# Relational graph layers on one core: sums kept relation by relation, read by TensorE from the ring, and the last node tile in a bank of its own

## The reference

```
agg = segment_sum(x[src], etype * N + dst)          # per relation and node, 8 x 3125 x 256
h   = relu( sum_r agg[r] @ W[l, r] + x @ root[l] + bias[l] )   # layers 1 and 2
h   = sigmoid( ... )                                 # layer 3
x   = x + h3 + linear_attention(layernorm(x))
x   = x + mixture_of_8_experts(layernorm(x), top 2)
```

## Time and profile before

| what | us |
|---|---|
| median of three runs | 3841.38 |
| the profiled execution | 3845.77 |
| its span, from the first to the last instruction | 3844.0 |
| TensorE busy | 3026.0 (79%) |
| GpSimd busy | 2399.1 (62%) |
| VectorE busy | 1830.8 (48%) |
| ScalarE busy | 689.2 (18%) |

### The profile page before, as it was taken

The page is one execution under the profiler, slowest core; times in us unless marked ns, Lnnn a source line. Parts: engine busy times, 40 slices in busy tenths (PEclk is TensorE's granted clock), DMA queues, the critical chain, the costliest instruction groups (busy, mean ns, idle before and its releaser), DMA issues.

```text
span 3844.0 us, 55574 instructions
## 1 busy us (share of the span) xinstructions
PE 3026.0 (79%) x15306; PEld 2475.6 (64%) x15307; DVE 1830.8 (48%) x3744; ACT 689.2 (18%) x1109; POOL 2399.1 (62%) x2536
## 2 busy tenths in 40 slices
PE   2888788888768888888888677877877884899991
PEld 2767667676657677776777566776766761566661
DVE  5455554554545555455454365565555542222222
ACT  0111111111111111111111122122222221222220
POOL 3777777777757777777776577777777755000005
PEclk9788988888978877788787788788878877899996
DMA  4333333433443333333333433333333325333334
GB/s 149 114 113 115 114 113 113 117 113 113 117 123 109 109 107 107 109 108 108 109 108 102 146 106 104 105 105 105 106 105 105 105 80 197 104 105 105 106 113 129
DMA packets 205784, 434.65 MB, mean 113 GB/s; under 512 B 51647, under 2 KB 115608, under 8 KB 205674
## 3 DMA queue, kind: packets, MB, share of 16 engines
q0 software_dynamic: 120864, 330.20, 30.0%
q1 hardware_dynamic: 81424, 102.07, 8.1%
q10 hardware_dynamic: 3386, 1.24, 0.1%
HBM read 398.24 MB, written 35.09 MB: 113 GB/s over the span
## 4 chain that ended last, share of the span: by engine, by line
POOL 46%; PE 22%; issue 21%; DMA 4%; DVE 3%; DVEq 1%; ACT 1%; SPq 1%; ACTq 0%; POOLq 0%
POOL arena L473 44%; PE bank L1293 7%; PE bank L1411 4%; PE bank L1438 4%; PE bank L1236 4%; DMA arena<-rows_dram,arena 2%; POOL xs_dram L507 1%; PE bank L1423 1%; POOL arena L518 1%; DMA hT_all<-in_L_ffn_b_dram 1%; PE bank L1231 1%; DVEq L973 1%; PE bank L1229 1%; DMA arena<-in_L_gnn_roots_dram 0%; DVE arena L987 0%
## 5 line engine op out<-in xcount | busy, mean ns | idle before, releaser
L473 POOL DMA_INDIRECT arena<-rows_dram,arena x2418 | 2289.9, 947 | 848.6 <-issue 783.2
L1293 PE MATMUL bank<-arena 128*128 128x128 f32 x9672 | 1756.4, 329 | 578.5 <-DVE arena L987 309.8
L1293 PEld LDWEIGHTS bank<-arena 128*128 128x128 f32 x9672 | 1526.3, 229 | 823.2 <-DVE arena L987 429.4
L987 DVE TENSOR_TENSOR arena<-arena,bank 128x256 f32 x2418 | 1019.2, 422 | 1385.6 <-PE bank L1293 1076.7
L1236 PE MATMUL bank<-arena 128*128 128x256 f32 x2400 | 612.6, 397 | 0.0
L1236 PEld LDWEIGHTS bank<-arena 128*128 128x128 f32 x2400 | 457.4, 203 | 52.0
L571 ACT COPY arena<-arena 128x1024 f32<-128x1024 f32 x150 | 300.8, 2053 | 607.1 <-DVE arena L928 308.1
L518 POOL DMA_INDIRECT arena<-ys_dram,pos x50 | 48.5, 969 | 511.0 <-DMA ys_dram<-arena 496.1
L958 DVE TENSOR_TENSOR arena<-bank,arena 128x1408 f32<-128x1408 f32 x222 | 355.9, 1604 | 15.4 <-issue 15.2
L1123 DVE TENSOR_TENSOR hT_all<-bank,hT_all 128x512 f32<-128x512 f32 x114 | 73.7, 687 | 342.6 <-DMA hT_all<-in_L_ffn_b_dram 284.8
L1411 PE MATMUL bank<-arena 128*128 x456 | 211.3, 607 | 11.7 <-issue 11.4
(11 more groups left out here) (188 smaller groups left out, 1100.6 us busy)
## 6 DMA issues: line engine op xcount, KB each, us to landing
arena<-rows_dram,arena POOLq DMA_INDIRECT x2418, 2.8
hT_all<-b_dram SPq DMA_DIRECT2D x58, 512.0 KB, 3.5
arena<-in_L_ffn_W_dram SPq DMA_DIRECT2D x16, 512.0 KB, 7.6
arena<-in_L_ffn_W_dram SPq DMA_DIRECT2D x8, 1024.0 KB, 13.6
arena<-xs_dram SPq DMA_DIRECT2D x59, 128.0 KB, 3.6
hT_all<-in_L_ffn_b_dram SPq DMA_DIRECT2D x58, 128.0 KB, 3.9
ys_dram<-arena SPq DMA_DIRECT2D x56, 128.0 KB, 1.7
rows_dram<-arena SPq DMA_DIRECT2D x50, 128.0 KB
```

The source lines that it names most:

```text
L473: nc.gpsimd.indirect_dma_start(out=gath[:, slot, :], out_offset=None, in_=rows_dram[l], in_offset=bass.IndirectOffsetOnAxis(ap=idx_ring[:, ...
L987: nc.vector.tensor_tensor(acc, acc, bank[EDGE_BANKS[u % 3]][:, 0:KD * WC].rearrange("p (k n) -> p k n", k=KD), ALU.add).then_inc(S["tile_a ...
L1293: mm = nc.tensor.matmul(bank[EDGE_BANKS[u % 3]][:, k * WC:(k + 1) * WC], gath[:, slot, k * P:(k + 1) * P], onehot[:, slot, :], start=True, ...
```

## The change

The ring is laid out relation by relation: `agg` is now `[k, relation, node]` with 256 + 16 nodes for each relation. TensorE takes a node tile's sums of one relation, 128 adjacent columns, as weights straight from the ring. `aggst` and its 150 copies go. VectorE's add goes to 16 runs of 16 columns (was 2 runs of 128), and the one-hot column of an edge is relation x 16 + offset in the window. The half is cleared when the node product is done (was: when the copies are made), at edge tile 17 (was 14). ScalarE copies the root input at edge tile 4 into one of two buffers. Pieces stand behind edge tiles 9 to 14 (were 12 to 17), in the last span behind 9 to 13 (were 10 to 13). Node tile 24's root input is copied at edge tile 11 of the last span, and its output goes to a bank of its own.

```
-READY, ZERO = 8, 14
+READY, ZERO = 8, 17
-STAGE, POST, TURN, BACK = READY, 19, 23, 26
-PIECES = {12: (0,), 13: (1,), 14: (2,), 15: (3,), 16: (4,), 17: (5,)}
-LAST_PIECES = {10: (0,), 11: (1, 2), 12: (3, 4), 13: (5,)}
+STAGE, LAST_STAGE, POST, TURN, BACK = 4, 11, 19, 23, 26
+PIECES = {9: (0,), 10: (1,), 11: (2,), 12: (3,), 13: (4,), 14: (5,)}
+LAST_PIECES = {9: (0, 1), 10: (2,), 11: (3,), 12: (4,), 13: (5,)}
...
-        agg_w = carve(KD * (RC + WC))
-        agg = agg_w.rearrange("p (k n) -> p k n", k=KD)
-        aggst_w = carve(KD * REL * P)
-        aggst = aggst_w.rearrange("p (k r n) -> p k r n", k=KD, r=REL)
+        agg_w = carve(KD * REL * RN)
+        agg = agg_w.rearrange("p (k r n) -> p k r n", k=KD, r=REL)
-        hT = carve(D)
+        hT = [carve(D) for _ in range(2)]
+        def place_of(t, par):
+            return P * (t % 2 if isinstance(t, int) else 1 - par)
+        def node_bank(t):
+            return bank[LAST_BANK if is_int(t, NT - 1) else NODE_BANK]
...
-                for k in range(KD):
-                    wait(act, "node_ready", NT * l + t + 1)
-                    wait_apart(act, "node_mm", NT * l + t)
-                    nc.scalar.copy(aggst[:, k, :, :], agg[:, k, at:at + TC].rearrange("p (n r) -> p r n", r=REL)).then_inc(S["stage_full"], 1)
+                wait_apart(act, "node_mm", NT * l + t - is_int(t, NT - 1))
+                nc.scalar.copy(hT[place_of(t, par) // P], tile_of(hT_all, t)).then_inc(S["h_staged"], 1)
...
                                 if u == STAGE:
-                                    stage_in(l, t, 0 if s.par else TC)
+                                    h_stage(l, t, s.par)
+                                if is_last(s) and u == LAST_STAGE:
+                                    h_stage(l, NT - 1, 0)
...
-            nc.vector.tensor_scalar(e_wini, e_wini, REL.bit_length() - 1, None, ALU.logical_shift_left).then_inc(S["edges_made"], 1)
-            link(nc.vector.tensor_scalar(e_win8, e_win, float(REL), None, ALU.mult))
-            nc.vector.tensor_tensor(e_loc, e_code, e_win8.unsqueeze(2).to_broadcast([P, EC, P]), ALU.subtract).then_inc(S["edges_made"], 1)
+            link(nc.vector.tensor_tensor(e_off, e_dstf, e_win.unsqueeze(2).to_broadcast([P, EC, P]), ALU.subtract))
+            nc.vector.scalar_tensor_tensor(out=e_loc, in0=e_typ, scalar=float(WN), in1=e_off, op0=ALU.mult, op1=ALU.add).then_inc(S["edges_made"], 1)
...
-                wait(dve, "stage_full", KD * (NT * l + t + 1))
-                nc.vector.memset(agg[:, :, at:at + TC], 0.0).then_inc(S["agg_zero"], 1)
+                wait(dve, "node_mm", NT * l + t + 1)
+                nc.vector.memset(agg[:, :, :, at:at + P], 0.0).then_inc(S["agg_zero"], 1)
...
-                                acc = agg[:, :, bass.ds(wins[j], WC)]
+                                acc = agg[:, :, :, bass.ds(wins[j], WN)]
...
                 if p == 0:
                     wait(pe, "h_staged", n + 1)
+                    if is_int(t, NT - 1):
+                        pe.wait_ge(S["qkv_out"], NT)
+                        wait(pe, "mctx_out", min(l, 1))
                     wait_apart(pe, "hn_made", n)
...
-                    if r == 0:
+                    if r == 0 and general:
                         wait_apart(pe, "stage_full", KD * n + k + 1)
-                    m = nc.tensor.matmul(o, aggst[:, k, r, :], wrel[:, k, r * D:(r + 1) * D], start=False, stop=c == CALLS - 1)
+                    elif c == 0:
+                        wait_apart(pe, "node_ready", n + 1)
+                    m = nc.tensor.matmul(o, agg[:, k, r, at:at + P], wrel[:, k, r * D:(r + 1) * D], start=False, stop=c == CALLS - 1)
```

More of the change, by code:

```diff
@@ L41 @@
 RING = 2 * P
-RC = RING * REL
+RN = RING + WN
 TC = P * REL
-READY, ZERO = 8, 14
+READY, ZERO = 8, 17
 SPAN_INV = -(-(1 << 16) // SPAN)
@@ L603, in hidden_rows @@
                 wait_apart(act, "node_mm", NT * l + t + 1)
-                nc.scalar.activation(hn, bank[NODE_BANK][:, 0:D], ACT.Relu).then_inc(S["hn_made"], 1)
+                nc.scalar.activation(hn, node_bank(t)[:, 0:D], ACT.Relu).then_inc(S["hn_made"], 1)
             def turned_back(l, t):
@@ L616, in sigmoid @@
                 wait_apart(act, "node_mm", NT * l + t + 1)
-                nc.scalar.activation(hn, bank[NODE_BANK][:, 0:D], ACT.Sigmoid).then_inc(S["hn_made"], 1)
+                nc.scalar.activation(hn, node_bank(t)[:, 0:D], ACT.Sigmoid).then_inc(S["hn_made"], 1)
             def deviation(t, n):
@@ L714, in general @@
                                 b = bank[GEN_BANKS[k][h]][:, :].rearrange("p (n r) -> p r n", r=REL)
-                                m = nc.scalar.copy(aggst[:, k, :, h * P // 2:(h + 1) * P // 2], b)
+                                m = nc.scalar.copy(agg[:, k, :, h * P // 2:(h + 1) * P // 2], b)
                             m.then_inc(S["stage_full"], 1)
@@ L973, in span @@
                             _, wins = nc.values_load_multi_w_load_instructions(
-                                win_row[0:1, bass.ds(SPAN * s.m + CH * a, tiles)], engines=(dve.engine,), min_val=0, max_val=RC - REL,
+                                win_row[0:1, bass.ds(SPAN * s.m + CH * a, tiles)], engines=(dve.engine,), min_val=0, max_val=RING - 1,
                                 skip_runtime_bounds_check_because="masked when they were made")
```

44 lines of the change are left out of this document (20 added, 24 removed).

## The result

The changed kernel takes 3831.5 us (median of 20 runs, 3828.27 to 3834.12) and the kernel before 3837.44 beside it (20 runs, 3833.85 to 3844.87): ratio 0.9983 [0.9977, 0.999]. Run again on another chip it was 0.998 [0.9971, 0.9989]. So the change makes the kernel faster by 5.9 us here and by 7.0 there (3840.04 to 3833.0), where 0.5 was forecast. The forecast time, 3841, lies 9.5 above the 3831.5. Of these, 3.9 are its starting point: the kernel before had a median of 3841.38 in three runs and has 3837.44 in twenty. The profiled execution took 3830.5, its span 3828.7. The profiled execution of the kernel before had been a long one (3845.77, over 8 above its median here), so most of the distance between these two traces is not the change's.

What follows compares the result with a forecast made beforehand. GpSimd's indirect gathers bound the layers, so edits show only at the start and layer ends. 0.86 - 0.2 x 2 - 0.8 x 2 + 0.3 x 2 = -0.5 us from 3841.38, forecast 3841, range 3832 to 3849.

Steps and rivals of the forecast that it cites:

- part 1: Inside the layers: removing the 150 staging copies (300.8 us of ScalarE) gives 0, since gathers cover them.
- B: Slower: VectorE's adds become the bound, 3950 us at 0.80 an add, chance 0.02; a mild form 3844, chance 0.08.
- C: Slower: VectorE's clearings in their new form shut GpSimd's gathers out, 122 us, to 3963; chance 0.02.
- D: Faster: the layers speed up because the copies are absent, to 3829; chance 0.02.
- Part 2: Setup: one more big VectorE operation, two small ones fewer, ahead of the first gather: +0.86 us.
- Part 3: End of the last edge span: tile 23's pieces start one edge tile earlier; 0 at first turn, -0.2 us at two others.
- Part 4: Between node tiles 23 and 24: the early root input copy removes a TensorE wait, -0.8 us at each of two turns.
- rival A: Faster: TensorE's clock holds behind tile 23's turning, 1.7 us a turn, perhaps 0.5 from earlier pieces, to 3837; chance 0.14.
- Part 5: Layer ends: clearing waits for the node product; 0 in layers one and two, +0.3 us twice in layer three.
- Parts 6 and 7: Adds in sixteen runs of 16 stay at 0.42 us; two more expert weight blocks load early; 0 each.

Runs made afterwards that it cites:

- the gap filled: Kernel before, with dummy products of zeros on TensorE between node tiles 23 and 24 in layers one and two: 3838.36 us, ratio 0.9999.
- the woven ones: Changed kernel with tile 24's products directly behind tile 23's: 3819.44 us (0.9955) without layer three's two end clearings, 3822.72 (0.9953) with them.
- the two single edits on the kernel before: Kernel before with only tile 24's root input copied early: 3838.81 us, 0.9994; with only the earlier last-span pieces: 3839.82 us, 1.0.

## Why the prediction was wrong

*The layers and part 1.* Right in what was said of tiles 0 to 22: no stretch of gathers changed, and copies kept as idle work cost nothing there. Rivals B, C and D fell: the add is 421 ns, the longest gather 1.190 us, and the layers did not speed up without the copies.

*Part 2, setup.* +0.86 forecast, +0.66 to +0.71 measured. The first of the big passes started at 25.52 instead of the assumed 25.70.

*Part 3, end of the last span.* The first failed step. "One tile's product only changes sides, 0" read an accident: in that one execution tile 9's gather was late. In the two further executions of before that gather was in time, the bias product stood 0.29 and 0.27 ahead of the last gather's start, and in the changed kernel it stands 1.53 and 1.56 ahead: 1.3 earlier. Against it stands tile 10's product, 0.45 woven in at the full clock, not the 0.58 to 1.16 I subtracted. So 0.8 at the full clock at each of three ends, where I had 0, 0.2 and 0.2: 2.4 instead of 0.4. It is not 0.8 every time: with the same pieces and the full clock, two other kernels built on the changed one ended tile 23's product 9.54 and 9.40 behind the last gather at the first turn, and not 8.9.

*Part 4, between the tiles.* The gap went from 1.99 to 1.00 (of it idle: 1.57 to 0.66), as forecast (-0.8 said, -1.0 measured). The second failed step is the sentence that the copies of tile 24's sums were no bound. They are: 0.21 us of waiting in the kernel before, and 0.85 as soon as the root copy is early. The only profile hid it, because the clock there had halved ahead of it. With the clock full, tile 24's product takes 9.08 with the copies and 8.66 without: 0.42 a turn more.

*The clock, rival A.* The third and largest step: the sum puts the clock at nothing, and I gave the rival that has it 0.14. It is what happened, at nearly the price I had put on it, and the sign that I had named for it, over 0.9 behind the turnings, was seen: 1.00. At the turns of the changed kernel the relation products take 7.07; in the three executions of before they take 7.83 to 8.83, with the root products stretched too in the first. Tile 24's product took 10.60 on the mean of the two further executions, 9.08 with the clock full: 1.5 a turn, 1.7 in the rival. Count the turns of layers one and two, over all kernels on the chips where the gathers set the pace. Where the gap between the two tiles' products was at most 1.0 us and TensorE did not wait for a copy afterwards, or had the gap filled, the clock held through tile 24's product at 14 turns of 14; with a gap of 2 us, or 1.0 and then 0.85 of waiting, it fell at 11 of 14. The other chip adds 6 of 6 held, and 1 of 2 fallen. Both numbers belong to the account: it is not certain to fall, but it never fell with the short gap. All that held with the long one were first turns, with the clock full through tile 23's product ahead of them. In layer three, where TensorE idles over 5 us there in every kernel but the woven ones, the clock over tile 24's product was 0.70 to 0.80, and 1.00 in the woven ones. My reason against it, that TensorE still idles for the activation, weighed too much. By the Trainium skill, "TensorE: Matmul & The Clock Gate", section "What's actually happening", the clock is gated by how busy TensorE has been; the counts above agree with its direction.

*Part 5, clearing.* Right in mechanism, half in size: +0.42 between tiles 23 and 24 and +0.78 behind tile 24, for 0.3 each. The clearing starts 0.50 behind the product and not 0.1, and 0.36 more comes behind it for a reason not found. The index copies, which I had set aside, did become the last thing that layer three's first gather waits for (27.38 us, ended by ScalarE), as the mixing adds now stand behind the clearing. It cost nothing that the table shows: 6.29 from tile 24's product to that gather, 6.76 before.

*Parts 6 and 7.* Right, 0 and 0.

Put together by size: pieces -2.4 (at the full clock), gap -2.0, copies -0.8, clock -3.1, clearing +1.2, setup +0.7 make -6.4. The forecast had -0.4, -1.6, 0, 0, +0.6, +0.9. That the sum fits a measured 5.9 to 7.0 doesn't prove each term: the two single edits on the kernel before show no gain in time, though both show it in the rows, and the clock's share rests on the rows of the filled gap and the counts of turns.

## What to carry to other kernels

Look for the turns between covered stretches, and price them at both clocks: a gap that looks worth 0.8 us was worth about 3 a turn with the copies' wait behind it, because the clock of the next 9 us went with it at most turns, and the slow clock itself hides the wait that comes next. A step that waits for two things gains little until both go. Take two or three traces before calling a wait absent, and give a buffer of its own an order that uses it: the last tile's own bank can give nothing, by the order of instructions, until its products are moved ahead of the turning, and then 10 us (3822.72 against 3833.0 on one chip).

## What was not expected of the hardware

The kernel before took 3837.4 to 3840.0 us (medians) in four sets and 4998.68 in a fifth, on another chip. There, in the traces of kernels built on either, a gather is the same 946 ns, and VectorE waited 947 us or more for what the trace does not name. The changed kernel is 0.2% faster in two of the four sets, and three variants built on it were over 1% slower there: which engine decides can differ by chip. And sixteen runs of 16 columns in SBUF cost VectorE no more than two of 128: 421 ns for 256 float32 columns, read from PSUM in one stretch.
